# Token attention on one core: scores from stacked parts replaced by three passes over 32 partitions, two row tiles and two column tiles at a time

## The chip, the cores and the metric

One core of a Trainium2 chip runs the whole program. The metric is the device time in microseconds, as the median of several runs. The engines are TensorE (PE; its weight loads are listed apart as PEld), VectorE (DVE), ScalarE (ACT), GpSimd (POOL) and SyncE (SP), which issues the DMA transfers.

## What is computed

The input x has 64 batches of 96 channels by 512 tokens. The first part, which the change touches, is attention over tokens:

```python
q, k, v = jnp.split(qkv, 3, axis=1)                # 32 channels each
weight = jnp.einsum('bct,bcs->bts', q * scale, k * scale)
weight = jax.nn.softmax(weight, axis=-1)
h = jnp.einsum('bts,bcs->bct', weight, v)
```

Then follow a layer norm, a grouped-query attention with rotary embedding over the 32 channels as a sequence, and a feed-forward block with ternary weights, each added to h. These two blocks take about two thirds of the time and are the same in both kernels.

## The kernel before, in words

Token attention works on 16 groups (NG) of 4 batches (GB). Each batch has a 512 x 512 matrix of scores, cut into 4 tiles of 128 x 512, so a group has 16 tiles (STEPS). Every tile is computed twice. A **row tile** (rows, L622 to L628) has queries as rows; DVE takes the maximum of each row (maximum, L472 to L475) into one column of row_max. A **column tile** (cols, L635 to L643) is the transposed tile, keys as rows; ACT takes exp of it (exps, L421 to L435) into the ring E. Its matmul also subtracts the maximum of each query, so the exponentials need nothing but a scale.

Scores must be nearly fp32-exact while TensorE multiplies fp32r. So q and k are split into a high part (ACT, raise_, L413) and a low part (POOL, lower, L368). For each batch, three parts of 32 channels are stacked on 96 partitions, (high, high), (high, low), (low, high), in QP for queries and KP for keys. One matmul over 96 partitions then gives the whole sum. The stacking is done by DMA: stack(g), L270 to L282, copies the parts into every third partition of QP and KP, six transfers of 256 KB a group. Two more partitions of QP, 96 and 97, get the negative maxima, again as high and low part (store_max, L289 to L296); the same two partitions of KP hold ones (L565). So a column tile is one matmul over 98 partitions.

The maxima of a group travel so: when all 16 row tiles are reduced, TensorE transposes row_max (transpose_maxima, L630), DVE splits the result in max_hi and max_lo (take_transposed, L477), and SP stores both into QP. cols(g, 0) waits for that.

TensorE follows an order written out by hand (step, L686): in each of 16 steps of group g one row tile of group g+1 or g+2 and one column tile of group g or g+1. LOOK = 7 row tiles of a group are made ahead. At four steps (OUT_AT) comes weigh(g, i), L645: the exponentials of four batches times v, as matmuls with 32 output columns for each batch. Once a group comes total(g), L656: the sums of the exponentials, four sums of pairs from POOL (sum_pair, L373) and eight tiles of E, again with 32 output columns each.

The row tiles, the transposed maxima and the totals share a ring of NS = 3 PSUM banks (S, score_ring): entry n may start when entry n - 3 has been read (enter_ring, L617). Column tiles use three banks of their own (ST): tile n waits for exponential n - 3. The two outputs use the other two banks.

DVE also turns the totals (turn_sums), inverts them (invert, L492) and multiplies the output (finish, L499), at three steps after a total, and from group 8 on makes the weights of the feed-forward block ternary (below, above, L93 to L102) behind tiles 3 and 5. ACT measures weights in the first half (L437, L442) and splits those of the second attention from group 9 on (attn_high, L79), with POOL for the low parts (attn_low, L87). SP's queue carries everything in its order: the stacking of group g+2, the load of v, the loads of weights, the load of q and k of group g+3, the store of h and the store of the maxima.

Of the kernel before, what the change touches and what calls it, by code (L numbers as in the profile page):

```python
# [121 lines left out]
LOOK, TAKE = 7, 1  # L122
MAX_AT = 2 + STEPS - LOOK
DEN_AT = STEPS + 3
MEASURES_AT = {"fold": (8, 5), "spread": (8, 9), "last_sum": (13, 5)}


def score_ring():

    entries = [("row", 0, k) for k in range(STEPS)]  # L130
    for k in range(LOOK):
        entries += [("row", 1, k)] + ([("max", 0)] if k == TAKE else [])
    for g in range(NG):
        for u in range(2, STEPS + 2):
            if u < MAX_AT and g + 1 < NG:
                entries.append(("row", g + 1, u - 2 + LOOK))
            if u >= MAX_AT and g + 2 < NG:
                entries.append(("row", g + 2, u - MAX_AT))
            if u == MAX_AT + TAKE and g + 1 < NG:
                entries.append(("max", g + 1))  # L140
            if u + STEPS == DEN_AT and g > 0:
                entries.append(("den", g - 1))
            entries += [(what, 0) for what, at in MEASURES_AT.items() if at == (g, u)]
    entries.append(("den", NG - 1))
    return {entry: n for n, entry in enumerate(entries)}
# [8 lines left out]
NB, NV, NE, NS, NO = 3, 2, 3 * GB, 3, 2  # L154


class TokenTiles:

    def __init__(self, sb):
        parts = {}  # L160
        for n in (1, 2):
            parts["q", n] = sb(f"q_parts{n}", [P, GB, T], F32R)
            parts["k", n] = sb(f"k_parts{n}", [P, GB, T], F32R)
        self.qk = sb("qk_split", [P, 4, T])
        VT = {0: sb("v_t0", [P, NT, P])}
        for of in ("q", "k"):
            parts[of, 0] = sb(f"{of}_parts0", [P, GB, T], F32R)
# [3 lines left out]
        self.QP, self.KP = [parts["q", n] for n in range(NB)], [parts["k", n] for n in range(NB)]  # L171
# [13 lines left out]
def token_attention(nc, block, sem, tiles, W, rows1, qk_raw, vt, h1, tables_in, norm_in, mask_in, ident_in, w_attn,  # L185
                    w_ffn):

    with ExitStack() as ctx:
# [3 lines left out]
        QP, KP, VT, qk, E, SUM = tiles.QP, tiles.KP, tiles.VT, tiles.qk, tiles.E, tiles.SUM  # L192
# [15 lines left out]
        stacked = [sem(f"t_stacked{n}") for n in range(2)]  # L208
# [14 lines left out]
        COPIES = 6 * DMA  # L223
        SPLIT_AT = 13
# [8 lines left out]
        OUT_AT = {8: 0, 10: 1, 13: 2, 17: 3}  # L233
        def staged(g):

            return E[:, NE - 4:NE, :] if g == 1 else qk[:, :, :]

        def split_raw(g):
            return staged(g)[:, 0:2, :]

        def split_high(g):
            return staged(g)[:, 2:4, :].bitcast(F32R)

        def split_low(g):
            return staged(g)[:, 0:2, :].bitcast(F32R)

        def copies(g):
            return COPIES * (g // 2 + 1)

# [12 lines left out]
        def _(sp):  # L262
            def load_qk(g):
                if g == 2:
                    sp.wait_ge(stacked[0], copies(0))
                elif g > 2:
                    sp.wait_ge(stacked[(g - 1) % 2], copies(g - 1))
                sp.dma_start(split_raw(g), qk_raw[g, :, :, :]).then_inc(qk_in[g % 2], DMA)

            def stack(g):  # L270
                p, done = g % NB, stacked[g % 2]
                if g >= NB:
                    sp.wait_ge(st_done, STEPS * (g - NB + 1))
                sp.wait_ge(hi_done, g + 1)
                high, low = split_high(g).bitcast(FP32), split_low(g).bitcast(FP32)
                sp.dma_start(QP[p][0:3 * CH:3, :, :].bitcast(FP32), high[:, 0, :]).then_inc(done, DMA)
                sp.dma_start(KP[p][0:3 * CH:3, :, :].bitcast(FP32), high[:, 1, :]).then_inc(done, DMA)
                sp.dma_start(QP[p][1:3 * CH:3, :, :].bitcast(FP32), high[:, 0, :]).then_inc(done, DMA)
                sp.dma_start(KP[p][2:3 * CH:3, :, :].bitcast(FP32), high[:, 1, :]).then_inc(done, DMA)
                sp.wait_ge(lo_done, g + 1)  # L280
                sp.dma_start(QP[p][2:3 * CH:3, :, :].bitcast(FP32), low[:, 0, :]).then_inc(done, DMA)
                sp.dma_start(KP[p][1:3 * CH:3, :, :].bitcast(FP32), low[:, 1, :]).then_inc(done, DMA)  # L282
# [6 lines left out]
            def store_max(g):  # L289
                for part, of in enumerate((max_hi, max_lo)):  # L290
# [4 lines left out]
                    row = QP[g % NB][3 * CH + part:3 * CH + part + 1, :, :].bitcast(FP32)  # L295
                    sp.dma_start(row, of[:, :].bitcast(FP32)).then_inc(max_in, DMA)  # L296
# [11 lines left out]
            def convert_ffn(c):  # L308
                if c == 6:
                    sp.wait_ge(stacked[(NG - 1) % 2], copies(NG - 1))  # L310
# [15 lines left out]
            stack(0)  # L326
            load_qk(2)
            stack(1)
            load_v(0)
# [6 lines left out]
            for g in range(NG):  # L336
                if g + 2 < NG:
                    stack(g + 2)
# [28 lines left out]
        def _(pool):  # L367
            def lower(g):  # L368
                pool.wait_ge(hi_done, g + 1)
                nc.gpsimd.tensor_tensor(split_low(g), split_raw(g), split_high(g).bitcast(FP32), ALU.subtract  # L370
# [16 lines left out]
            for g in range(3):  # L387
                lower(g)
            for g in range(NG):
# [11 lines left out]
                if g + 3 < NG:  # L401
                    lower(g + 3)
# [1130 lines left out]
```

## Time and profile before

| | |
|---|---|
| Median of 3 runs | 1083.79 us (1079.22 to 1084.54) |
| The profiled execution: its own time | 1077.4 us |
| Its span, first to last instruction | 1075.6 us |
| PE busy in the span | 972.6 us (90%) |
| DVE / ACT / POOL busy | 736.6 / 446.2 / 497.7 us |
| Mean granted clock of TensorE | 0.976 |
| DMA moved | 113.07 MB |
| Token attention | from the start to about 332 us |

Times are in microseconds from the start of the span unless marked ns. In a timeline each line has the start, the busy time, engine, line of the kernel, operation, what is written from what, and the number of instructions merged into it; in brackets the idle time of the engine before it and who ended it. Successive matmuls overlap, so the distance between two starts is the cost of one in a stream, and its duration is how long it takes to end.

### The profile page before, as it was taken

How to read it: one execution, taken by the hardware profiler on the slowest of the kernel's cores; microseconds unless marked ns; L12 is line 12 of the kernel's file. 1: busy time of each engine (PE TensorE's matmuls, PEld its weight loads, DVE VectorE, ACT ScalarE, POOL GpSimd, SP SyncE). 2: the span in 40 equal slices, each digit the busy share in tenths (PEclk: the TensorE clock that was granted, in tenths of full speed). 3: DMA queues.
4: the chain of work that ended last, by engine and by line, in shares of the span. 5: the costliest groups of instructions: out<-in, count | busy, mean ns of one | idle time of the engine just before them, and what ended most of it. 6: DMA issues, size and time to landing. Idle time of an engine off the chain costs nothing. (4 is left out here: it accounts for less than half of the span.)

```text
span 1075.6 us, 20479 instructions
## 1 busy us (share of the span) xinstructions
PE 972.6 (90%) x7799; PEld 525.5 (49%) x7799; DVE 736.6 (68%) x1262; ACT 446.2 (41%) x761; POOL 497.7 (46%) x376
## 2 busy tenths in 40 slices
PE   4998999888887598999999999999999999999976
PEld 2433333333322245556566465564655656646545
DVE  5676758888797756567676685676856766668542
ACT  1677866677674522323333233232332333323311
POOL 2243434476677743634554355344553455435500
PEclk9999999999989699999999999999999999999998
DMA  8988886675524222322223123222232222322300
GB/s 220 268 289 229 284 248 186 192 212 180 171 94 112 51 59 44 80 49 54 69 49 78 49 49 80 48 67 59 54 78 51 51 68 49 78 52 46 73 16 21
DMA packets 157478, 113.07 MB, mean 105 GB/s; under 512 B 126336, under 2 KB 126976, under 8 KB 157440
## 3 DMA queue, kind: packets, MB, share of 16 engines
q1 hardware_dynamic: 157440, 112.59, 38.8%
q8 instruction: 21, 0.34, 0.1%
q14 instruction: 17, 0.14, 0.0%
HBM read 49.36 MB, written 8.39 MB: 54 GB/s over the span
## 5 line engine op out<-in xcount | busy, mean ns | idle before, releaser
L1007 POOL TENSOR_TENSOR roped<-rope_cos,rope_sin 128x512 f32<-128x512 f32 x80 | 100.8, 1268 | 222.1 <-DVE rope_sin L1173 222.1
L475 DVE TENSOR_REDUCE row_max<-score_rows 128x1 f32<-128x512 f32 x256 | 162.7, 677 | 46.8 <-PE score_rows L627 46.6
L435 ACT ACTIVATE exps<-score_cols 128x512 f32<-128x512 f32 x256 | 139.7, 600 | 82.8 <-PE score_cols L642 81.0
L1360 PE MATMUL ffn_sum<-x_hi,ffn_w 128*128 128x128 f16 x1408 | 165.0, 222 | 7.9 <-DMA x_lo<-x_lo_rows 7.9
L1361 PE MATMUL ffn_sum<-x_lo,ffn_w 128*128 128x128 f16 x1408 | 164.8, 222 | 0.0
L627 PE MATMUL score_rows<-k_parts,q_parts 96*128 96x512 f32 x256 | 120.1, 484 | 28.1 <-DMA k_parts<-qk_split 14.3
L1360 PEld LDWEIGHTS ffn_sum<-x_hi,ffn_w 128*128 128x128 f16 x1408 | 139.6, 99 | 11.7 <-DMA x_lo<-x_lo_rows 8.3
L1361 PEld LDWEIGHTS ffn_sum<-x_lo,ffn_w 128*128 128x128 f16 x1408 | 140.1, 99 | 1.8
L642 PE MATMUL score_cols<-q_parts,k_parts 98*128 98x512 f32 x256 | 107.3, 427 | 13.2 <-DMA q_parts<-max_lo 8.8
L379 POOL TENSOR_TENSOR exp_sums<-exps 128x512 f32<-128x512 f32 x64 | 83.3, 1330 | 57.7 <-PE score_rows L627 38.0
L627 PEld LDWEIGHTS score_rows<-k_parts,q_parts 96*128 96x128 f32 x256 | 51.4, 202 | 116.4 <-DVE row_max L475 65.4
L1019 POOL TENSOR_TENSOR roped_lo_rows<-roped,roped_hi_rows 128x512 f16<-128x512 f32 x80 | 94.5, 1197 | 15.7 <-ACT roped_hi_rows L1093 15.7
L1418 PE MATMUL proj<-attn_slots,ctx_hi 128*128 128x512 f16 x256 | 97.1, 379 | 3.5 <-POOL attn_slots L90 2.7
L1419 PE MATMUL proj<-attn_slots,ctx_hi 128*128 128x512 f16 x256 | 97.3, 380 | 0.0
L1295 DVE SCALAR_TENSOR_TENSOR h<-proj,o_unscale,h_res 128x512 f32<-128x512 f32 x16 | 12.0, 751 | 120.2 <-PE proj L1423 120.2
L852 POOL TENSOR_TENSOR rstd<-var,minus_half 128x1 f32<-128x1 f32 x32 | 23.7, 739 | 133.2 <-DVE var L847 133.2
L1073 ACT ACTIVATE squares<-ffn_sum 128x512 f32<-128x512 f32 x32 | 19.1, 597 | 149.2 <-PE ffn_sum L1309 149.2
L1307 PE MATMUL proj<-attn_slots,x_hi 128*128 128x512 f16 x192 | 73.5, 383 | 3.6 <-DMA x_lo<-x_lo_rows 3.6
L652 PE MATMUL tok_out<-exps,v_t 128*32 128x512 f32 x512 | 70.5, 624 | 3.5 <-ACT exps L435 3.4
L1308 PE MATMUL proj<-attn_slots,x_hi 128*128 128x512 f16 x192 | 73.5, 383 | 0.0
L1309 PE MATMUL proj<-attn_slots,x_lo 128*128 128x512 f16 x192 | 73.4, 382 | 0.0
L90 POOL TENSOR_TENSOR attn_slots<-attn_slots 128x1024 f16<-128x1024 f32 x20 | 47.3, 2364 | 52.5 <-ACT attn_slots L85 52.5
(153 smaller groups left out, 1931.1 us busy)
## 6 DMA issues: line engine op xcount, KB each, us to landing
q_parts<-qk_split SPq DMA_DIRECT2D x45, 256.0 KB, 4.2
k_parts<-qk_split SPq DMA_DIRECT2D x45, 256.0 KB, 4.7
attn_slots<-in_w_attn SPq DMA_DIRECT2D x20, 512.0 KB, 7.1
ffn_w<-in_w_ffn SPq DMA_DIRECT2D x13, 704.0 KB, 8.4
qk_split<-in_qk SPq DMA_DIRECT2D x15, 512.0 KB, 5.9
raw_ffn<-in_w_ffn SPq DMA_DIRECT2D x8, 704.0 KB, 5.3
v_t<-in_v_t SPq DMA_DIRECT2D x16, 256.0 KB, 5.7
h_rows<-tok_out_sum SPq DMA_DIRECT2D x16, 256.0 KB, 4.9
```

The source lines that it names most:

```text
L379: nc.gpsimd.tensor_tensor(SUM[:, b, :], E[:, first, :], E[:, second, :], ALU.add).then_inc(summed, 1)
L435: nc.scalar.activation(E[:, n % NE, :], ST[n % 3][:, :], ACT.Exp, scale=TOK_SCALE).then_inc(exp_done, 1)
L475: nc.vector.reduce_max(row_max[:, g % 2, k:k + 1], S[n % NS][:, :], AX.X).then_inc(s_free, 1)
L627: nc.tensor.matmul(bank[:, :], QP[g % NB][0:3 * CH, b, t * P:(t + 1) * P], KP[g % NB][0:3 * CH, b, :], start=True, stop=True).then_inc(s_f ...
L642: nc.tensor.matmul(ST[n % 3][:, :], KP[g % NB][0:3 * CH + 2, b, i * P:(i + 1) * P], QP[g % NB][0:3 * CH + 2, b, :], start=True, stop=True) ...
L1007: nc.gpsimd.tensor_tensor(rope[:, c, :], ra[c % 2][:, :], rb[c % 2][:, :], ALU.add).then_inc(added, 1)
L1019: nc.gpsimd.tensor_tensor(rope_lr[:, c, :], rope[:, c, :], rope_hr[:, c, :], ALU.subtract).then_inc(r_lo, 1)
L1307: nc.tensor.matmul(dst, ah, bh, start=(i == 0), stop=False)
L1360: nc.tensor.matmul(dst, w, x2h[:, k, :], start=(k == 0), stop=False)
L1361: ins = nc.tensor.matmul(dst, w, x2l[:, k, :], start=False, stop=(k == KD - 1))
L1418: nc.tensor.matmul(PROJ[1][:, :], ch[:, k, :], W.hi(at, D), start=(k == 0), stop=False)
L1419: nc.tensor.matmul(PROJ[1][:, :], ch[:, k, :], W.lo(at, D), start=False, stop=False)
```

## The change

- q and k are loaded with the 4 batches of a group on 32 partitions each (partition 32 b + channel), where before a partition held one channel of one batch in another order. The stacking, its tiles and its semaphore go. High and low parts stay in their own tiles, `high` and `low`, three of each in turn.
- A score tile is three accumulating matmuls over the 32 partitions of its batch: high x high, high x low, low x high. A column tile gets a fourth matmul over two partitions that adds the negative maxima: ones_r as weights, neg_max as the moving operand. The maxima are stored by DMA into partitions 0 and 1 of each batch's 32 in neg_max, which has two buffers.
- TensorE works in 8 windows a group instead of 16 steps. A window takes two row tiles of two neighbouring batches and two column tiles of the other two batches, and issues pass by pass over the four tiles. The waits for all four come ahead of the first matmul. The rings keep their three banks.
- Ahead of the column tiles are 8 row tiles (AHEAD = 4 pairs) instead of 7. The maxima of a group are transposed in window 5, the column tiles of the next group begin in window 8; weighings stand in windows 4, 5, 6 and, for the group before, 1; the total of the group before in window 2. The row tiles' order over batches changes with row_tile.
- ACT's raise and POOL's lower of a group come one group later than before (g+2 instead of g+3), behind exponential 3 and ahead of the sums. E has 16 tiles instead of 12. The raw q and k have two buffers.

```diff
+PAIRS = STEPS // 2
+AHEAD = PAIRS // 2
+MAX_AT, OUT_AT, DEN_AT = AHEAD + 1, {4: (0, 0), 5: (0, 1), 6: (0, 2), 1: (1, 3)}, 2
+def row_tile(j):
+    pair, second = divmod(j, 2)
+    i, half = divmod(pair, 2)
+    return 2 * half + second, i
+def rows_beside(g, w):
+    g, pair = (g + 1, w - 1 + AHEAD) if w < MAX_AT else (g + 2, w - MAX_AT)
+    return (g, pair) if g < NG else None
+def cols_at(g, w):
+    g, pair = (g, w) if w < PAIRS else (g + 1, 0)
+    return (g, pair) if g < NG else None
...
             def load_qk(g):
-                if g == 2:
-                    sp.wait_ge(stacked[0], copies(0))
-                elif g > 2:
-                    sp.wait_ge(stacked[(g - 1) % 2], copies(g - 1))
-                sp.dma_start(split_raw(g), qk_raw[g, :, :, :]).then_inc(qk_in[g % 2], DMA)
-            def stack(g):
...
+                if g >= 2:
+                    sp.wait_ge(lo_done, g - 1)
+                sp.dma_start(raw(g), qk_raw[g, :, :, :]).then_inc(qk_in[g % 2], DMA)
...
             def store_max(g):
+                if g >= 2:
+                    sp.wait_ge(st_done, STEPS * (g - 1))
...
-                    row = QP[g % NB][3 * CH + part:3 * CH + part + 1, :, :].bitcast(FP32)
-                    sp.dma_start(row, of[:, :].bitcast(FP32)).then_inc(max_in, DMA)
+                    sp.dma_start(neg_max[g % 2][part::CH, :].bitcast(FP32), of[:, :].bitcast(FP32)).then_inc(max_in, DMA)
...
             def raise_(g):
                 act.wait_ge(qk_in[g % 2], DMA * (g // 2 + 1))
...
+                if g >= NB:
+                    act.wait_ge(st_done, STEPS * (g - NB + 1))
+                nc.scalar.copy(high[g % NB][:, :, :], raw(g)).then_inc(hi_done, 1)
...
-            def rows(g, k):
...
-                nc.tensor.matmul(bank[:, :], QP[g % NB][0:3 * CH, b, t * P:(t + 1) * P], KP[g % NB][0:3 * CH, b, :],
-                                 start=True, stop=True).then_inc(s_full, 1)
+            def split_score(bank, g, b, i, of, n):
+                q, k = (0, 1) if of == "rows" else (1, 0)
+                p, at = g % NB, of_batch(b)
+                part, other = ((high, high), (high, low), (low, high))[n]
+                return nc.tensor.matmul(bank, part[p][at, q, i * P:(i + 1) * P], other[p][at, k, :], start=(n == 0),
+                                        stop=(of == "rows" and n == 2))
+            def scores(row_pair, col_pair):
+                rows, cols = [], []
+                if row_pair is not None:
+                    g, pair = row_pair
+                    if pair == 0:
+                        pe.wait_ge(lo_done, g + 1)
+                    for j in (2 * pair, 2 * pair + 1):
+                        rows.append((enter_ring(ring["row", g, j])[:, :], g, *row_tile(j)))
+                if col_pair is not None:
+                    g, pair = col_pair
+                    if pair == 0:
+                        pe.wait_ge(max_in, 2 * DMA * (g + 1))
+                    for u in (2 * pair, 2 * pair + 1):
+                        n = STEPS * g + u
+                        if n >= 3:
+                            pe.wait_ge(exp_done, n - 2)
+                        cols.append((ST[n % 3][:, :], g, u % GB, u // GB))
+                for n in range(3):
+                    for bank, g, b, i in rows:
+                        ins = split_score(bank, g, b, i, "rows", n)
+                        if n == 2:
+                            ins.then_inc(s_full, 1)
+                    for bank, g, b, i in cols:
+                        split_score(bank, g, b, i, "cols", n)
+                for bank, g, b, i in cols:
+                    of = slice(b * CH, b * CH + 2)
+                    nc.tensor.matmul(bank, ones_r[of, :], neg_max[g % 2][of, :], start=False, stop=True
+                                     ).then_inc(st_done, 1)
...
+            def step(g, w):
+                scores(rows_beside(g, w), cols_at(g, w))
+                if w == MAX_AT and g + 1 < NG:
                     transpose_maxima(g + 1)
+                if w in OUT_AT:
+                    back, i = OUT_AT[w]
+                    if g - back >= 0:
+                        weigh(g - back, i)
+                if w == DEN_AT and g > 0:
                     total(g - 1)
```

## Rows read from the trace of the kernel before

**Rows 1.** Waits of the whole span: engine, line, waited for; total, times, longest.
```profile
ACT exps L435 <- PE score_cols L642: 81.0, 64, 12.9
...
PEld score_rows L627 <- DVE row_max L475: 65.4, 100, 1.8
...
PEld score_cols L642 <- DMA q_parts<-max_lo: 17.4, 16, 2.5
```

**Rows 2.** Two windows: length, busy by engine, granted clock, DMA share, GB/s.
```profile
103.00:121.00 18.00, 17.07 (x102) 7.03 (x105) 13.15 (x24) 13.85 (x26) 7.37 (x5) 1.00 0.90 278
...
139.00:158.00 19.00, 16.41 (x81) 6.68 (x77) 12.53 (x22) 11.83 (x22) 7.37 (x5) 0.91 0.84 262
```

**Rows 3.** Timeline, TensorE: first column tiles of groups 0, 7, 15; one later matmul.
```profile
31.73 1.22 PE L642 MATMUL score_cols<-q_parts,k_parts 98*128 98x512 f32 x2 [1.95 <-DMA q_parts<-max_lo]
...
152.78 0.80 PE L642 MATMUL score_cols<-q_parts,k_parts 98*128 98x512 f32 x1 [1.85 <-DMA q_parts<-max_lo]
...
156.19 0.50 PE L627 MATMUL score_rows<-k_parts,q_parts 96*128 96x512 f32 x1
...
306.28 1.19 PE L642 MATMUL score_cols<-q_parts,k_parts 98*128 98x512 f32 x2 [1.41 <-ACT exps L435]
```

**Rows 4.** Timeline of group 4, TensorE and its weight loads.
```profile
102.15 0.19 PEld L627 LDWEIGHTS score_rows<-k_parts,q_parts 96*128 96x128 f32 x1
...
102.39 0.40 PE L627 MATMUL score_rows<-k_parts,q_parts 96*128 96x512 f32 x1
...
102.62 0.40 PE L642 MATMUL score_cols<-q_parts,k_parts 98*128 98x512 f32 x1
...
103.84 1.90 PE L664 MATMUL score_rows<-exps,tok_ones 128*32 128x512 f32 x16
...
105.67 0.50 PE L627 MATMUL score_rows<-k_parts,q_parts 96*128 96x512 f32 x1
...
111.10 0.39 PE L642 MATMUL score_cols<-q_parts,k_parts 98*128 98x512 f32 x1
...
112.42 0.50 PE L627 MATMUL score_rows<-k_parts,q_parts 96*128 96x512 f32 x1
...
117.00 0.50 PE L642 MATMUL score_cols<-q_parts,k_parts 98*128 98x512 f32 x1 [0.18 <-DMA q_parts<-max_lo]
```

**Rows 5.** DMA issues: count, KB each, median time to landing.
```profile
q_parts<-qk_split SPq DMA_DIRECT2D x45, 256.0 KB, 4.2
```

**Rows 6.** Lines of token attention, 0 to 340: count, busy us, mean ns, idle before.
```profile
L475 DVE TENSOR_REDUCE row_max<-score_rows 128x1 f32<-128x512 f32 x256 | 162.7, 677 | 46.8 <-PE score_rows L627 46.6
...
L435 ACT ACTIVATE exps<-score_cols 128x512 f32<-128x512 f32 x256 | 139.7, 600 | 82.8 <-PE score_cols L642 81.0 <-POOL exp_sums L379 0.6
...
L379 POOL TENSOR_TENSOR exp_sums<-exps 128x512 f32<-128x512 f32 x64 | 83.3, 1330 | 57.7 <-PE score_rows L627 38.0 <-ACT exps L435 14.8 <-PE score_rows L673 4.9
...
L84 ACT ACTIVATE attn_slots<-attn_slots,w_scale 128x1024 f16<-128x1024 f32 x16 | 18.3, 1146 | 7.7 <-POOL attn_slots L90 7.7
...
L101 DVE SCALAR_TENSOR_TENSOR ffn_w<-raw_ffn,w_thr,ffn_w 128x1408 f16<-128x1408 f32 x7 | 16.3, 2322 | 0.0
...
L96 DVE TENSOR_SCALAR ffn_w<-raw_ffn,w_nthr 128x1408 f16<-128x1408 f32 x7 | 10.1, 1448 | 0.0
```

**Rows 7.** Timeline of group 4, DVE.
```profile
107.02 0.23 DVE L494 RECIPROCAL tok_rden<-tok_den_t 128x16 f32<-128x16 f32 x1
...
107.92 0.65 DVE L475 TENSOR_REDUCE row_max<-score_rows 128x1 f32<-128x512 f32 x1
...
108.50 0.67 DVE L504 TENSOR_TENSOR tok_out_sum<-tok_out,tok_den_t 128x512 f32<-128x512 f32 x1
...
114.16 0.27 DVE L482 TENSOR_SCALAR max_hi<-score_rows 16x128 fp32r<-16x128 f32 x1
```

**Rows 8.** Timeline of the start, POOL and TensorE.
```profile
5.32 2.35 POOL L370 TENSOR_TENSOR qk_split<-qk_split 128x1024 fp32r<-128x1024 f32 x1 [4.88 <-ACT qk_split L419]
...
14.34 9.52 PE L627 MATMUL score_rows<-k_parts,q_parts 96*128 96x512 f32 x16 [14.34 <-DMA k_parts<-qk_split]
```

More of the change, by code:

```diff
@@ L151, in shares @@
     return [range(end - count, end) for count, end in zip(counts, ends)]
-NB, NV, NE, NS, NO = 3, 2, 3 * GB, 3, 2
+NB, NV, NE, NS, NO = 3, 2, STEPS, 3, 2
 class TokenTiles:
     def __init__(self, sb):
-        parts = {}
+        high, low, VT = {}, {}, {}
         for n in (1, 2):
[L162 to L167, printed above, removed]
+            high[n], low[n] = sb(f"qk_high{n}", [P, 2, T], F32R), sb(f"qk_low{n}", [P, 2, T], F32R)
+            if n == 1:
+                sb("tok_spare", [P, 4, T])
+        self.neg_max = [sb(f"neg_max{n}", [P, T], F32R) for n in range(2)]
+        self.ones_r = sb("tok_ones_r", [P, P], F32R)
+        sb("tok_spare2", [P, 2 * T - P])
+        self.qk = sb("qk_raw", [P, 4, T])
+        VT[0] = sb("v_t0", [P, NT, P])
+        high[0], low[0] = sb("qk_high0", [P, 2, T], F32R), sb("qk_low0", [P, 2, T], F32R)
         self.E = sb("exps", [P, NE, T])
@@ L170, in __init__ @@
         VT[1] = sb("v_t1", [P, NT, P])
-        self.QP, self.KP = [parts["q", n] for n in range(NB)], [parts["k", n] for n in range(NB)]
+        self.high, self.low = [high[n] for n in range(NB)], [low[n] for n in range(NB)]
         self.VT = [VT[n] for n in range(NV)]
@@ L232, in token_attention, with raw, of_batch @@
         SUMS_BEFORE = [sum(GB * d for d in DEPTH[:g]) for g in range(NG + 1)]
[L233 to L248, printed above, removed]
+        def raw(g):
+            return qk[:, 2 * (g % 2):2 * (g % 2) + 2, :]
+        def of_batch(b):
+            return slice(b * CH, (b + 1) * CH)
         def ffn_stage(c):
@@ L385, in sum_third @@
                 nc.gpsimd.tensor_tensor(SUM[:, b, :], SUM[:, b, :], E[:, third, :], ALU.add).then_inc(summed, 1)
-            for g in range(3):
-                lower(g)
+            lower(0)
+            lower(1)
             for g in range(NG):
+                if g + 2 < NG:
+                    lower(g + 2)
                 for c in A_CONVERTED[g][:1]:
@@ L445, in sum_ffn @@
                                      ).then_inc(f_stat, 1)
-            for g in range(3):
-                raise_(g)
+            raise_(0)
+            raise_(1)
             exps(0, 0)
@@ L471, in _, with maximum @@
         def _(dve):
-            def maximum(g, k):
-                n = ring["row", g, k]
+            def maximum(g, j):
+                n = ring["row", g, j]
+                b, i = row_tile(j)
+                k = b * NT + i
                 dve.wait_ge(s_full, n + 1)
```

152 lines of the change are left out of this document (49 added, 103 removed).

## The prediction

> **What bounds it now.** I read first the waits, then the windows, then the costs of one instruction, and last the timeline of one group. The waits show no single master: the loads of row tiles wait 65.4 us for DVE's maxima, the exponentials wait 81.0 us for TensorE's column tiles, and TensorE waits on the row of maxima that a DMA brings (17.4 us on the weight load) [rows 1]. The windows show a full machine: in 18 us of one group TensorE has records for 17.07 us, ACT for 13.85, DVE for 13.15, and the DMA engines are busy 0.90 [rows 2]. The stage is thus a loop of three engines with TensorE a little ahead. Its pace: the first column tile of group 0 starts at 31.73, that of group 7 at 152.78, that of group 15 at 306.28 [rows 3]: 17.3 us a group over seven groups, then 19.2 over eight.
>
> In the timeline, scores follow each other every 0.235 us at full clock (102.39 to 102.62), and the next weights are loaded meanwhile. One lasts 0.40, or 0.50 after an idle moment, so 0.10 of its load is then exposed. A weighing (eight records) adds 112.42 - 111.10 - 0.235 = 1.08, a total adds 105.67 - 102.62 - 0.235 = 2.82 [rows 4]. TensorE's own work per group is so 32 x 0.235 + 4 x 1.08 + 2.82 + 0.24 (the transposition, one pitch, an estimate) = 14.9 of 17.3 us. The tiles of 32 output columns share TensorE: 16 records in 1.90 us [rows 4]; rows of 32 partitions side by side are not in this trace.
>
> **The change, part by part.**
>
> 1. Copies. 96 transfers of 256 KB leave SP's queue, 25 MB in all [rows 5]. TensorE's waits on DMA inside the stage are mostly for the maxima, which stay. ACT's raise and POOL's lower keep their size. Lower now stands before the sums, which cost 4 x 1330 ns [rows 6]; they have until step 2 of the next group, four windows or over 8 us, so I cost that at nothing. Without that cover it is 2.4 us a group. SP's new wait for the column tiles of a group that is long finished, before the store of the maxima, costs nothing; so does ACT's before the raise.
>
> 2. Passes. Four tiles need 3 rounds of four matmuls plus one round of two that adds the maxima, where there were 4 matmuls of 0.235. If the four row groups run side by side, a window (two row tiles, two column tiles) is 0.10 + 4 x 0.235 = 1.04 us, against 0.94. That is no saving, and per group 0.8 us more. Lower bound for a round: 0.235; upper: four or two matmuls one after another, 14 x 0.235 = 3.29 a window. I take the lower, since the nearest row, with column tiles, shows four at once.
> The Trainium skill (TensorE: Matmul & The Clock Gate, Part 3) gives 3.07 times for four row tiles of 512 columns instead of 4; by that a round would be an estimated 0.31 and the sum some 37 us longer. It also says that weight loads overlap running matmuls only in other row groups; the load at 102.15 inside a matmul over the same rows disagrees.
>
> 3. Coupling, the term that decides. The rings stay at three banks, but a window takes two of each. Its second tile may start only when the first tile of the window before has been reduced, and the same holds for the exponentials. Before, a ring of three let TensorE run ahead by a tile at a time. In a window begun at 0: row tiles are full at 0.50 + 2 x 0.235 = 0.97, column tiles, one round later, at 1.21. With handovers of 0.04 to 0.05 (107.02 + 0.23 to the next, an estimate for all [rows 7]) the first maximum (677 ns [rows 6]) frees TensorE at 1.74 and the first exponential (600 ns) at 1.90. A plain window takes 1.90, not the 0.94 that TensorE used before. With a weighing TensorE is the limit: 2.12. With a total: 3.86.
>
> 4. DVE in windows 3 and 4. The inversion takes 0.90 of DVE (107.02 to 107.92) and the finish 0.60, the pitch of the maximum before it (107.92 to 108.50) [rows 7]; they now stand between tiles 12 and 13 and behind 13. From window 3's start: tile 12 at 1.01, inversion, tile 13 at 2.53, finish, tile 14 at 3.75, done 4.42. Window 5 starts at 4.5 rather than 4.02.
> A group: 2.12 + 3.86 + 4.5 + (2.12 + 0.23) + 2.12 + 1.90 + 1.90 = 18.75.
> The maxima: taken about 2.5 us into window 5; store and landing took 117.00 - 114.43 = 2.6 [rows 4, 7]; window 8 begins 6.4 after window 5, so that wait (17.4 us on the weight loads [rows 1]) should vanish. The sum has it already, since 18.75 holds no such wait.
>
> 5. Late groups 8 to 13. DVE's two conversions (1448 and 2322 ns [rows 6]) follow tiles 3 and 5, each the last of a pair. TensorE has only one window in hand, so they hold windows 8 and 1: by the same steps 1.95 us. ACT's two conversions (two operations of 1146 ns each [rows 6]) behind tiles 3 and 12 add about 0.4: 21.1 a group.
>
> 6. Start. The lowering of group 0 ends at 5.32 + 2.35 = 7.7 and rows start there rather than at 14.34. But TensorE is at half clock then (16 tiles in 9.52 us, DVE-paced, 0.60 apart [rows 8]). A pair at that clock: 0.79 + 2 x 0.43 = 1.65 to full, 0.7 for the maximum and its handovers: 2.4. Twelve pairs: 28.8, so first columns at 36.5 instead of 31.73, +5.
>
> Sum: +5; groups 0 to 6: 7 x 18.75 - 121.05 = +10; one more for the first group at half clock; groups 7 to 14: 2 x 18.75 + 6 x 21.1 - 153.5 = +11; the last group is bounded by ACT and DVE in both, 0. That is +27 us at full clock.
>
> 7. Clock. At 152.78, after 1.85 us without work, a matmul takes 0.80; at 156.19 one takes 0.50 again [rows 3], and that stretch has a granted clock of 0.91 (the other shown 1.00) [rows 2]: 3.4 us at the lower of the two levels, 1.2 and 2.4 GHz. In plain windows TensorE now streams 0.94 of 1.90 us, two or three in a row. I take one such fall a group, at 1.2 us on the path: +18. Ends: 0, or two falls wholly on the path, +50.
>
> Total +45: 1077.4 + 45 = 1122. The profiled run is 6.4 below the median 1083.79, so 1129 beside the median; I say 1128. The bounds of steps 3 and 7 reach from +15 to +90.
>
> **Rivals.**
>
> A. Forecast, slower by 2 to 7%: 0.60.
>
> B. The row groups don't run fully side by side: loads of the same array rows, or outputs into four banks, serialize. With rounds of 0.43 (each load of 0.19 exposed [rows 4]) a window grows by some 0.65, 5 us a group, 1128 + 80 = 1208; wholly serial, 2.35 a window less the idle 0.9 where there is some, 16 a group: 1128 + 250 = 1380. By the skill's 3.07, 1165. For: no row shows four row groups. Against: the column tiles. Chance 0.18 (0.08 up to 1195, 0.10 above). In this rival the change doesn't do what "side by side" says.
>
> C. Faster. The copies are what holds the stage (DMA 0.90 busy), so that with them gone no engine waits and TensorE's own work decides. Its price per group is then 8 x 1.04 + 4 x 1.08 + 2.82 + 0.24 = 15.7; against 17.3 and 19.2 (there DVE keeps it near 17.5), and a start some 6 us earlier: -11 - 14 - 6 = -31, about 1053. It decides if plain windows take under 1.5 us. For: the DMA share, the waits on maxima. Against: in the timeline the engines wait for each other, not for a copy, and the ring needs the first maximum. Chance 0.13.
>
> D. No change: DVE and ACT are a tenth quicker with less traffic and the clock holds: a plain window of 1.7, 17.6 a group, the start's loss made good: 1084. Chance 0.09.
>
> **Numbers.** A measurement of this kernel can tell about 0.5% from no change (1078.4 to 1089.2). Faster 0.13, same 0.09, slower 0.78. The range 1080 to 1195 leaves out C (0.13) and the upper part of B (0.10), a little over 2 in 10; A's own range is 1098 to 1165.
>
> **What would show it.** Step 1: the q_parts and k_parts issues gone, DMA share near 0.6. Step 2: matmuls of 32 rows starting some 10 ns apart in fours, rounds 0.235 apart. Step 3: starts of plain windows 1.9 apart, idle of TensorE put down to exponentials rather than maxima, and column tiles of neighbouring groups 18 to 19 us apart early, 21 late. Step 4: tile 14 of a group waits behind the finish. Step 6: first columns near 36.5. Step 7: PEclk under 0.95 in slices 2 to 12. The forecast is wrong if rounds are over 0.3 apart (B) or if the stage's column tiles end before 320 (C).

## The result, and the profile after

The changed kernel takes 1142.12 us (median of 4 runs, 1139.12 to 1145.1) beside 1082.01 for the kernel before on the same chip: a ratio of 1.0556, 95% interval 1.0514 to 1.0598. It is slower by 60 us, where 45 were forecast, within the range. The profiled execution has a span of 1140.5 us against 1075.6.

The page of the changed kernel: span, busy tenths of TensorE, its granted clock and the DMA share in 40 slices.

```profile
span 1140.5 us, 23159 instructions
...
PE   4788888887778967999999999999999999999986
...
PEclk9999899788887587999999999999999999999998
DMA  3235351233114231322322312322322322222210
```

The granted clock is below 9 tenths in ten of the first sixteen slices (mean of the span 0.943, before 0.976), and 88 MB are moved instead of 113. The first slices need care: the granted clock of the start reads 1.00,

```profile
0.00:36.09 36.09, 18.42 (x69) 9.81 (x69) 14.51 (x26) 3.37 (x3) 4.86 (x6) 1.00 0.37 130
```

but the durations of its matmuls (0.79, and rounds 0.43 apart) are those of the lower level until 53.5. In the start the level is therefore read from durations. The waits, answering to [rows 1]:

```profile
ACT exps L423 <- PE score_cols L651: 169.6, 108, 31.3
...
PEld score_rows L621 <- DVE row_max L465: 125.3, 96, 2.5
...
PE score_rows L621 <- ACT exps L423: 31.6, 36, 1.7
```

ACT now waits 169.6 us for column tiles instead of 81.0, the row tiles' weight loads wait 125.3 us for maxima instead of 65.4, and a wait is there that had no such row: row tiles that wait 31.6 us for exponentials. A window needs both rings. The pace, against [rows 3], by the first column tiles of groups 0, 7 and 15:

```profile
36.09 0.79 PE L621 MATMUL score_cols<-qk_high 32*128 32x512 f32 x2
...
177.45 0.50 PE L621 MATMUL score_cols<-qk_high 32*128 32x512 f32 x2
...
364.29 0.79 PE L621 MATMUL score_cols<-qk_high 32*128 32x512 f32 x2 [1.70 <-ACT exps L423]
```

| | before | after | difference |
|---|---|---|---|
| first column tile, group 0 | 31.73 | 36.09 | +4.4 |
| groups 0 to 6 | 121.05 (17.3 each) | 141.36 (20.2 each) | +20.3 |
| groups 7 to 14 | 153.50 (19.2 each) | 186.84 (23.4 each) | +33.3 |
| group 15 and all that follows | 769.3 | 776.2 | +6.9 |

The last line is the rest of each span. Its 6.9 are +11.4 in group 15, whose last pair of column tiles starts at 390.74, 26.5 us after its first (before 321.38, 15.1 us after), and -4.5 behind it.

One group in the timeline of TensorE, windows 3 and 4 of a group, and its last windows and the next window 1:

```profile
125.31 0.50 PE L621 MATMUL score_rows<-qk_high 32*128 32x512 f32 x2
125.32 0.50 PE L621 MATMUL score_cols<-qk_high 32*128 32x512 f32 x2
125.65 0.39 PE L621 MATMUL score_rows<-qk_low,qk_high 32*128 32x512 f32 x1
...
126.12 0.40 PE L651 MATMUL score_cols<-neg_max,tok_ones_r 2*128 2x512 f32 x2
127.30 0.49 PE L621 MATMUL score_rows<-qk_high 32*128 32x512 f32 x2 [0.78 <-ACT exps L423]
...
128.43 1.07 PE L666 MATMUL tok_out<-exps,v_t 128*32 128x512 f32 x8
129.89 0.49 PE L621 MATMUL score_rows<-qk_high 32*128 32x512 f32 x2 [0.39 <-DVE row_max L465]
...
136.35 0.50 PE L621 MATMUL score_rows<-qk_high 32*128 32x512 f32 x2 [0.78 <-ACT exps L423]
...
138.33 0.51 PE L621 MATMUL score_rows<-qk_high 32*128 32x512 f32 x2 [0.76 <-ACT exps L423]
...
138.92 0.63 PE L621 MATMUL score_cols<-qk_high,qk_low 32*128 32x512 f32 x2
...
139.90 1.94 PE L666 MATMUL tok_out<-exps,v_t 128*32 128x512 f32 x8
141.77 0.73 PE L621 MATMUL score_rows<-qk_high 32*128 32x512 f32 x2
```

Row and column tiles start within 0.01 us, the next round 0.34 later and the one for the maxima 0.81 later, as three rounds of 0.235 and the 0.10 that the first load adds. The window from 125.31 to 127.30 is a plain one: 1.99. Two more stand at 136.35 and 138.33, 1.98 apart. In the second the clock falls, after two idle stretches of TensorE of 0.78 and 0.76: a matmul lasts 0.63 and rounds are 0.43 apart, the weighing takes 1.94 instead of 1.07, until 0.73 at 141.77 is the last long one. DVE in the same group, against [rows 7]:

```profile
126.31 0.69 DVE L465 TENSOR_REDUCE row_max<-score_rows 128x1 f32<-128x512 f32 x1
126.92 0.24 DVE L484 RECIPROCAL tok_rden<-tok_den_t 128x16 f32<-128x16 f32 x1
...
127.83 0.65 DVE L465 TENSOR_REDUCE row_max<-score_rows 128x1 f32<-128x512 f32 x1
128.41 0.67 DVE L494 TENSOR_TENSOR tok_out_sum<-tok_out,tok_den_t 128x512 f32<-128x512 f32 x1
129.00 1.27 DVE L465 TENSOR_REDUCE row_max<-score_rows 128x1 f32<-128x512 f32 x2
```

The inversion (126.92) stands between the maxima of tiles 12 and 13 and the finish (128.41) behind 13; tile 14 comes at 129.00, and window 5 starts at 129.89, 4.58 after window 3, not when the weighing of window 4 is over (128.43 + 1.0). The windows of groups without and with a fall, and of the last group:

```profile
97.60:116.60 19.00, 16.30 (x173) 7.13 (x169) 12.85 (x22) 13.99 (x25) 7.38 (x5) 1.00 0.42 151
116.60:137.20 20.60, 17.88 (x175) 7.52 (x169) 12.85 (x22) 13.06 (x23) 7.38 (x5) 0.92 0.44 164
364.20:392.80 28.60, 27.00 (x120) 10.30 (x120) 14.67 (x22) 12.68 (x20) 14.11 (x9) 0.56 0.28 70
```

19.0 us at full clock, 20.6 with a fall (0.92), and in the last group a granted clock of 0.56 with TensorE 94% busy. By the distance of first column tiles, group 0 took 22.7 us (at the lower level until 53.5), groups 1 to 3 took 19.0, groups 4 to 7 20.5, and groups 8 to 14 between 21.4 and 26.1.

### The profile page after: what moved, and what is told of

It reads as the page before. It is cut to its first block and busy times, and to the rows that moved or that the text cites. A ratio compares the mean times of both kernels' runs of the same rounds, so it can differ in the third digit from the quotient of the medians.

```text
span 1140.5 us, 23159 instructions
## 1 busy us (share of the span) xinstructions
PE 1017.8 (89%) x9079; PEld 549.2 (48%) x9079; DVE 730.8 (64%) x1260; ACT 448.5 (39%) x761; POOL 487.7 (43%) x376
## 3 DMA queue, kind: packets, MB, share of 16 engines
HBM read 49.36 MB, written 8.39 MB: 51 GB/s over the span
## 5 line engine op out<-in xcount | busy, mean ns | idle before, releaser
L465 DVE TENSOR_REDUCE row_max<-score_rows 128x1 f32<-128x512 f32 x256 | 165.5, 683 | 106.6 <-PE score_rows L621 104.9
L423 ACT ACTIVATE exps<-score_cols 128x512 f32<-128x512 f32 x256 | 140.3, 595 | 169.8 <-PE score_cols L651 169.6
L621 PE MATMUL score_rows<-qk_high 32*128 32x512 f32 x256 | 73.7, 563 | 70.4 <-ACT exps L423 31.6
L362 POOL TENSOR_TENSOR qk_low<-qk_raw,qk_high 128x1024 fp32r<-128x1024 f32 x16 | 38.0, 2379 | 181.4 <-ACT qk_high L409 181.4
L621 PEld LDWEIGHTS score_rows<-qk_high 32*128 32x128 f32 x256 | 29.5, 209 | 167.4 <-DVE row_max L465 125.3
L666 PE MATMUL tok_out<-exps,v_t 128*32 128x512 f32 x512 | 85.4, 746 | 1.2 <-ACT exps L423 1.2
L861 POOL TENSOR_TENSOR rstd<-var,minus_half 128x1 f32<-128x1 f32 x32 | 22.7, 710 | 133.4 <-DVE var L856 133.4
L1082 ACT ACTIVATE squares<-ffn_sum 128x512 f32<-128x512 f32 x32 | 19.1, 597 | 151.8 <-PE ffn_sum L1318 151.8
L621 PE MATMUL score_cols<-qk_high 32*128 32x512 f32 x256 | 72.2, 560 | 3.2 <-ACT exps L423 3.2
```

The lines of the kernel that those rows point to most:

```text
L423: nc.scalar.activation(E[:, n % NE, :], ST[n % 3][:, :], ACT.Exp, scale=TOK_SCALE).then_inc(exp_done, 1)
L465: nc.vector.reduce_max(row_max[:, g % 2, k:k + 1], S[n % NS][:, :], AX.X).then_inc(s_free, 1)
L621: return nc.tensor.matmul(bank, part[p][at, q, i * P:(i + 1) * P], other[p][at, k, :], start=(n == 0), stop=(of == "rows" and n == 2))
L666: last = nc.tensor.matmul(OUT[g % NO][b * CH:(b + 1) * CH, :], VT[g % NV][:, i, b * CH:(b + 1) * CH], E[:, (STEPS * g + GB * i + b) % NE, ...
```

## The experiments

Every run stands beside runs of the kernel before on the same chip (medians 1076.6 to 1080.7), so runs from different chips are compared by ratio; the changed kernel has 1.0556. What is said of single groups rests on one trace of each kernel.

### The clock

Extra matmuls, which change nothing in the output, into the output bank that is free until the next weighing:

```diff
+            def fill(g, count):
...
+                if g >= NO:
+                    pe.wait_ge(h_done, g - NO + 1)
+                for _ in range(count):
+                    nc.tensor.matmul(OUT[g % NO][:, :], ones_r[:, 0:P], ones_r[:, :], start=True, stop=True)
...
                 scores(rows_beside(g, w), cols_at(g, w))
+                if w in (7, 8):
+                    fill(g + 1, 3)
+                if w == 3 or g == 0 and w < 3:
+                    fill(g, 3)
...
                 scores((0, pair), None)
+                fill(0, 3)
```

> The changed kernel with extra matmuls into an output bank that is free at that time (three of 512 columns, weights and operand all ones, behind the windows of the start, behind windows 7, 8 and 3, and 1 and 2 of the first group); what is computed stays the same. Theory: the clock fell once a group because TensorE idles 0.9 of 1.98 us in plain windows, and it was low through the start for the same reason. Then the granted clock of token attention is near 1.0, early groups take 19.0 instead of 20.5 us, a pair of the start 1.8 instead of 2.5, the first column tiles start near 29 instead of 36; in all 1110 (1100 to 1122) against 1142. Rival: the low stretches are hidden behind DVE and ACT, or the extra matmuls cost what they give: only the start gains, 1133 or more.

Measured: 1117.55, ratio 1.0362 (1.0314 to 1.0411). Every group from 1 to 7 took 19.1 us, without a fall. But the start got longer. Its timeline, and for comparison that of the changed kernel:

```profile
7.73 0.79 PE L621 MATMUL score_rows<-qk_high 32*128 32x512 f32 x2 [7.73 <-POOL qk_low L362]
...
9.30 1.65 PE L660 MATMUL tok_out<-tok_ones_r 128*128 128x512 f32 x3
10.88 0.79 PE L621 MATMUL score_rows<-qk_high 32*128 32x512 f32 x2
...
14.03 0.79 PE L621 MATMUL score_rows<-qk_high 32*128 32x512 f32 x2
```

```profile
8.18 0.79 PE L621 MATMUL score_rows<-qk_high 32*128 32x512 f32 x2 [8.18 <-POOL qk_low L362]
...
10.57 0.79 PE L621 MATMUL score_rows<-qk_high 32*128 32x512 f32 x2 [0.75 <-DVE row_max L465]
...
13.09 0.79 PE L621 MATMUL score_rows<-qk_high 32*128 32x512 f32 x2 [0.87 <-DVE row_max L465]
```

A pair takes 3.15 us with the extra matmuls and 2.49 without. TensorE had no pause between 7.73 and 14.03, and yet every duration is that of the lower level, and stays so until past 62 us (53.5 in the changed kernel). So "it idles, hence the low clock", as the expectation had it for the start, is refuted there: the first column tiles came at 45.78, where 29 was expected. The same without them in the start:

> As the kernel with extra matmuls, but none in the start (there the clock stayed low in spite of them, and a pair took 3.15 instead of 2.49 us): only behind windows 7, 8 and 3, and 1 and 2 of the first group. Theory (one fall of the clock a group in the plain windows, another stretch in the last group): 10 less than with them in the start, 1107 (1103 to 1112). Rival (what that kernel gained came from the clock having been raised in the start): the falls come back, 1125 or more.

Measured: 1112.03, ratio 1.0322 (1.0283 to 1.0361). Two windows of it, an early and a late group:

```profile
99.00:118.10 19.10, 18.77 (x184) 8.43 (x178) 12.84 (x22) 13.99 (x25) 7.40 (x5) 1.00 0.44 149
255.90:277.20 21.30, 18.98 (x184) 8.64 (x178) 16.87 (x25) 14.81 (x23) 11.60 (x8) 1.00 0.33 119
```

No fall in either, nor in any other group. Against 1.0556 the falls are worth some 25 us, and rather more, since the extra matmuls have a cost of their own (19.1 against 19.0 in a group without a fall). The first group stays long, 24.1 us. In the two traces the falls are worth 1.4 to 1.5 in each of groups 4 to 7, 19 in groups 8 to 14 together, and 10 in the last one alone, which shrank from 26.5 to 16.4 us.

### The pairs and the rings

One output bank (control), the bank that is freed so given to the row ring, and the same bank given to the column tiles. The control has NO = 1. The second run has NS = 4 besides, the third NST = 4, the number of banks for column tiles. The edit of the third run:

```diff
-NB, NV, NE, NS, NO = 3, 2, STEPS, 3, 2
+NB, NV, NE, NS, NO = 3, 2, STEPS, 3, 1
+NST = 4
...
-        ST = [pb(f"score_cols{n}") for n in range(3)]
+        ST = [pb(f"score_cols{n}") for n in range(NST)]
...
-                nc.scalar.activation(E[:, n % NE, :], ST[n % 3][:, :], ACT.Exp, scale=TOK_SCALE).then_inc(exp_done, 1)
+                nc.scalar.activation(E[:, n % NE, :], ST[n % NST][:, :], ACT.Exp, scale=TOK_SCALE).then_inc(exp_done, 1)
...
-                        if n >= 3:
-                            pe.wait_ge(exp_done, n - 2)
-                        cols.append((ST[n % 3][:, :], g, u % GB, u // GB))
+                        if n >= NST:
+                            pe.wait_ge(exp_done, n - NST + 1)
+                        cols.append((ST[n % NST][:, :], g, u % GB, u // GB))
```

> The changed kernel with one output bank instead of two, a control for the next two. The weighing of window 4 now waits until DVE has finished the group before, about 1 us after it would start. Both theories: 0.5 to 1.5 us a group and something at the end, 1155 (1145 to 1170).

> One output bank, and the freed bank goes to the ring of row tiles: four instead of three, so a window of row tiles needs only that the window before the last has been reduced. Theory (coupling of pairs to the ring): plain windows stay at 1.98 since the exponentials free them, but window 4 no longer waits for the finish and the late groups no longer wait for the two conversions: 10 to 25 us less than with one output bank alone. Rival (TensorE's own rounds or the clock set the pace): within 4 us of it.

> One output bank, and the freed bank goes to the column tiles: four instead of three. Theory: plain windows are freed by the first maximum then, 1.78 instead of 1.98, four or so a group: 8 to 14 us less than with one output bank alone; in the last group, which has column tiles only, TensorE alone sets the pace. Rival (TensorE's own rounds or the clock set the pace): within 4 us of it.

Measured: the control 1149.12, with four row banks 1124.77, with four column banks 1138.92, all on one chip and beside 1079.09. The row bank gives 24 us, the column bank 10. Of the 24, about 10 are the start: the first round for the maxima of column tiles comes at 27.3 us instead of 37.2. The column bank does what was expected in plain windows, and loses in late groups. Two window starts of the kernel with four column banks in the timeline of TensorE, and one late group in the windows:

```profile
63.56 0.50 PE L622 MATMUL score_rows<-qk_high 32*128 32x512 f32 x2
...
65.37 0.51 PE L622 MATMUL score_rows<-qk_high 32*128 32x512 f32 x2 [0.60 <-DVE row_max L466]
```

```profile
242.80:269.00 26.20, 22.03 (x173) 9.13 (x169) 15.81 (x25) 14.89 (x23) 10.75 (x7) 0.74 0.26 97
```

The window is 1.81 instead of 1.98, the first maximum now being what frees it. A late group takes 26.2 us with a clock of 0.74. Both banks moved the time by as much as the coupling theory said, and neither could have if TensorE's rounds were the bound.

The reverse: the kernel before, with nothing but waits added.

```diff
+            def ahead(g, u):
+                at = (g + 1, u - 2 + LOOK) if u < MAX_AT else (g + 2, u - MAX_AT)
+                if at[0] < NG:
+                    pe.wait_ge(s_free, ring[("row",) + at] - NS + 1)
+                n = STEPS * g + u
+                if n < STEPS * NG and n >= 3:
+                    pe.wait_ge(exp_done, n - 2)
             def step(g, u):
+                if u % 2 == 0:
+                    ahead(g, u + 1)
```

> The kernel before with waits added alone: ahead of every second step TensorE also waits for what the next step needs, so that it moves by two row and two column tiles as the changed one does; matmuls, copies and rings as before. Theory (moving by pairs in rings of three banks costs time by itself): a plain pair takes 1.43 instead of 0.94 us, less than the 1.98 of the changed kernel since its tiles end one after another; a group grows by 0.5 to 1.5 us, 1079 to 1095 (1087 to 1103). Rival (the coupling costs nothing; the fourth round and the clock are the whole loss): within 4 of 1079.

Measured: 1131.56, ratio 1.0552 (1.0471 to 1.0633): as slow as the change, with the old matmuls, the old copies and stacks. The expectation, 1095 and at most 1103, was 37 us short.

A pair of row tiles and the next in the timeline of TensorE, and the window of an early group:

```profile
111.65 0.50 PE L627 MATMUL score_rows<-k_parts,q_parts 96*128 96x512 f32 x1
...
113.93 0.47 PE L627 MATMUL score_rows<-k_parts,q_parts 96*128 96x512 f32 x1 [1.07 <-DVE row_max L475]
```

```profile
157.50:177.90 20.40, 17.85 (x91) 7.14 (x89) 12.91 (x22) 13.16 (x24) 7.58 (x6) 0.92 0.78 243
```

The pair begun at 111.65 holds until 113.93, 2.28 us, where 1.43 were expected. The profile names a maximum that had long been done; what ended last is an exponential, since ACT had a bound and its raise (110.78 to 113.23 in its timeline) around the exponential before. In a ring that TensorE fills tile by tile such a piece of work is absorbed; waiting for two at once it is not. And this kernel too has a fall of the clock in every group from 1 to 13, as in the window above (0.92), where the kernel before has three in the whole stage. Its granted clock is 0.955; how much of its 55 us is clock was not tried. All of them are lost in groups 0 to 14: the first column tile starts at 31.5, and the last group takes 14.9, both as before.

### The rounds

One pass instead of three, so that the low parts of the scores are left out:

```diff
-                part, other = ((high, high), (high, low), (low, high))[n]
-                return nc.tensor.matmul(bank, part[p][at, q, i * P:(i + 1) * P], other[p][at, k, :], start=(n == 0),
+                return nc.tensor.matmul(bank, high[p][at, q, i * P:(i + 1) * P], high[p][at, k, :], start=True,
...
-                for n in range(3):
+                for n in (2,):
```

> The changed kernel with one of the three passes (high times high) and the round for the maxima: two rounds a window instead of four; the scores leave out the low parts. Theory (the window is a chain: rounds, then the first maximum or exponential, then the next window): every round taken away shortens plain windows by its 0.235, 1.98 to 1.5, a pair of the start from 2.49 to 1.65, a group from 20.5 to 16 or so; in all 1077 (1065 to 1100). Rival (DVE and ACT set the pace and the rounds hide behind them): 1120 or more.

Measured: 1110.77, ratio 1.0331 (1.0283 to 1.0378): 24 us by ratio, not 65. Two window starts, and a late group:

```profile
123.43 0.50 PE L620 MATMUL score_rows<-qk_high 32*128 32x512 f32 x2 [0.76 <-ACT exps L423]
...
124.95 0.49 PE L620 MATMUL score_rows<-qk_high 32*128 32x512 f32 x2 [0.78 <-ACT exps L423]
```

```profile
247.70:271.10 23.40, 18.17 (x109) 5.24 (x105) 16.32 (x25) 14.94 (x24) 11.80 (x8) 0.67 0.28 108
```

The plain window did shrink to 1.52, and the start by 10 us. But TensorE, with less to do, was at the lower level for longer: granted clock 0.911 over the span, 0.67 in a late group of 23.4 us, and 0.76 from the first to the last column tile, where the changed kernel has 0.88. That the clock took what the missing rounds gave fits these rows, but it is argued and not shown, since this kernel was not tried with the extra matmuls.

The same matmuls with the three passes of a tile one behind the other in the queue:

```diff
-                for n in range(3):
-                    for bank, g, b, i in rows:
+                for bank, g, b, i in rows:
+                    for n in range(3):
...
-                    for bank, g, b, i in cols:
+                for bank, g, b, i in cols:
+                    for n in range(3):
```

> The changed kernel with the same matmuls in another order: the three passes of one tile, then those of the next, so that neighbours in the queue use the same 32 rows. Theory (four row groups really work at once, and the queue is served in order): ten rounds instead of four, a window of 2.45 instead of 1.04 us of TensorE, some 6 us more a group, 1240 (1215 to 1265). Rival (the records only start together and the work is the same): within 10 of 1142.

Measured: 1154.33, ratio 1.0738 (1.0698 to 1.0779). The theory's 100 us are not there, and the time is 12 us above 1142, just outside what the rival gave. The records show that the order in the queue was not the order of work:

```profile
153.54 0.51 PE L621 MATMUL score_rows<-qk_high 32*128 32x512 f32 x2
153.56 0.51 PE L621 MATMUL score_cols<-qk_high 32*128 32x512 f32 x2
153.88 0.39 PE L621 MATMUL score_rows<-qk_low,qk_high 32*128 32x512 f32 x2
...
154.12 0.40 PE L621 MATMUL score_rows<-qk_high,qk_low 32*128 32x512 f32 x2
```

In the queue the first tile's three passes stand ahead of all the others. On the engine the first passes of all four tiles start together, within 0.04 us from 153.54, then the second passes, then the third: the second tile's first matmul ran ahead of the first tile's second. Groups 1 to 3 take 19.1 us, about as before. By its trace the 12 to 20 us are lost in late groups above all (groups 7 to 14 took 198.6 us instead of 186.8), whose clock fell for longer; that cause is not settled.

This gives a remedy: if order in the queue doesn't matter, each tile's waits can stand ahead of its own matmuls.

```diff
                     for j in (2 * pair, 2 * pair + 1):
...
+                        bank = enter_ring(ring["row", g, j])[:, :]
+                        for n in range(3):
+                            ins = split_score(bank, g, *row_tile(j), "rows", n)
+                        ins.then_inc(s_full, 1)
...
                         if n >= 3:
                             pe.wait_ge(exp_done, n - 2)
...
+                        bank, b = ST[n % 3][:, :], u % GB
+                        for part in range(3):
+                            split_score(bank, g, b, u // GB, "cols", part)
...
```

> The changed kernel with the matmuls tile by tile, and each tile's waits ahead of its own matmuls instead of all waits ahead of the window (matmuls and rings as in the changed kernel; the run with the tiles one after another in the queue showed that TensorE still runs them side by side, if nothing waits between them). Theory (the loss is that a window waits for four banks at once): a tile starts when the tile three before it has been read, as in the kernel before; a pair of the start takes 1.6 instead of 2.5 us, a group 1.5 to 2.5 less; 1100 (1080 to 1118). Rival (the fourth round and the clock are the loss, or waits between tiles keep them from running side by side): 1145 or more.

> The same with the extra matmuls behind windows 7, 8 and 3 (and 1 and 2 of the first group). Theory: coupling and clock are separate losses, so that this takes off another 15 to 30: 1080 (1065 to 1098), near the kernel before. Rival (they are one loss: with the waits apart TensorE has no idle stretch that lowers the clock): within 6 of the run without them.

Measured: 1132.91, ratio 1.0496 (1.0454 to 1.0538), and with the extra matmuls 1106.54, ratio 1.0237 (1.0177 to 1.0298).

```profile
92.50:111.20 18.70, 18.70 (x174) 10.03 (x171) 12.84 (x23) 14.10 (x25) 7.39 (x5) 1.00 0.44 152
254.60:279.30 24.70, 22.93 (x172) 11.03 (x170) 16.80 (x25) 14.85 (x24) 11.55 (x8) 0.79 0.27 102
```

The first expectation, 1100, failed by 33 us. The start did what was expected: three row tiles every 2.43 us, 1.62 a pair, and the first maxima round at 28.0 instead of 37.5. But that is all that was gained. Groups 2 to 7 take 18.6 without a fall, 0.4 less than 19.0 where 1.5 to 2.5 were expected, and late ones take 24.7 at a clock of 0.79. The first two row tiles of a window 8 show why:

```profile
90.97 0.39 PE L621 MATMUL score_rows<-qk_high 32*128 32x512 f32 x1
91.20 0.40 PE L621 MATMUL score_rows<-qk_low,qk_high 32*128 32x512 f32 x1
91.44 0.39 PE L621 MATMUL score_rows<-qk_high,qk_low 32*128 32x512 f32 x1
91.65 0.50 PE L621 MATMUL score_rows<-qk_high 32*128 32x512 f32 x1
```

The tile starts at 90.97, 1.06 us after window 7 instead of 1.98, but the other three wait for their banks, and it has its three rounds to itself, as long as those of four tiles. The next starts at 91.65. By the start of window 2 little is left of the lead: window 1, again with a lone tile, takes 2.96 instead of 2.13, and windows 7, 8 and 1 together take 5.82 instead of 6.08. TensorE now has records for all of the 18.70 us and is by them the limit. Tiles that start one by one lose the side-by-side work that makes three passes as cheap as one.

The extra matmuls take off 26, within the 15 to 30 expected, so the two losses are separate; but the 1080 was missed by 27 as the run without them missed its 1100. With the extra matmuls the records fill all 19.1 us of an early group, so that less of them might do better. No kernel tried here beats the one before.

### Two smaller steps

The copies, put back for 12 groups into a tile that nobody reads:

> The changed kernel with the six copies a group put back for 12 of 16 groups (256 KB each, into a tile that nobody reads, from SP's queue at their old place). Theory (the copies were hidden): 1142 (1136 to 1149). Rival (the copies slowed the other engines or the loads, and the change gained something by leaving them out): 1155 or more.

Measured: 1138.47, ratio 1.0569 (1.0529 to 1.061), against 1.0556: 72 transfers, 19 MB, are worth nothing that can be measured in the changed kernel, where nothing on TensorE waits for them.

DVE's inversion and finish moved out of window 3's pair, in the kernel with extra matmuls:

```diff
-                    if j == row_before("den") + 1 and r >= 2:
+                    if j == row_before("den") + 2 and r >= 2:
                         invert(r - 2)
-                    if j == row_before("den") + 2 and r >= 2:
+                    if j == row_before("den") + 4 and r >= 2:
                         finish(r - 2)
```

> The changed kernel with extra matmuls behind windows 7, 8 and 3 (its early groups took 19.1 us each, with no fall of the clock), and on DVE the inversion moved from behind row tile 12 to behind 13 and the finish from behind 13 to behind 15: no work of DVE stands inside window 3's pair any more. Theory (the inversion and the finish hold window 5 by half a microsecond): early groups 18.6 to 18.7, in all 5 to 8 less than the 1112 without the move. Rival (window 5 is freed by the exponentials and TensorE's weighing anyway): groups stay at 19.1.

Measured: every group from 1 to 7 took 18.7 instead of 19.1 us, as expected. One of them:

```profile
96.70:115.40 18.70, 18.70 (x179) 8.43 (x178) 12.81 (x23) 13.97 (x26) 7.41 (x5) 1.00 0.43 153
```

In all it is 1111.42, ratio 1.0271 (1.0221 to 1.0322), and that interval reaches the 1.0322 of the kernel without the move, so the total doesn't show the gain. In the trace the last group took 21.2 instead of 16.4 us, with a fall of the clock that the other kernel has not; the extra matmuls do not keep the clock up there in every kernel.

## Why the prediction was right, by its steps

1. **Copies at nothing: right.** Their return cost nothing measurable, and the lowering ahead of the sums delayed nobody: window 2 with its total took 3.85 in an early group, the 3.86 of the sum. The DMA share fell further than the 0.6 that was named as a sign, to 0.42.
2. **Rounds: right.** Four row groups work side by side, 0.235 a round. The 3.07 times that the Trainium skill (TensorE: Matmul & The Clock Gate, Part 3) gives would have made rounds of an estimated 0.31; the trace has 0.23. The same part of the Trainium skill has the rule that weight loads overlap only with other row groups' matmuls, and it did not hold here either, as in the rows before: a round of 0.235 would have no room for a load of 0.19 in the same rows if the load had to wait. Rival B is out.
3. **Coupling: right in mechanism and size.** Plain windows 1.98 (forecast 1.90), early groups 19.0 at full clock (18.75), and window by window 2.13, 3.85, 1.98 + 2.59, 2.35, 2.13, 1.97, 1.98 against 2.12, 3.86, 4.5, 2.35, 2.12, 1.90, 1.90. One more row bank and one more column bank moved the time as this step says, and so did the waits added to the kernel before, which cost far more than worked out. Waits by tile did so in the start alone. Both sides of the coupling are thus needed for the account: four tiles must start together for the passes to be cheap, and rings of three banks do not let four start together without waiting.
4. **DVE in windows 3 and 4: right.** 0.4 us a group, by the run that moves it.
5. **Late groups: right at full clock.** In the kernel with extra matmuls behind the windows alone, without falls, groups 8 to 13 took 19.9 to 22.1 us, 21.0 on average; forecast 21.1. Group 14 took 20.9, where the forecast had 18.75, and no run takes the two conversions apart.
6. **Start: right, in part by luck.** 36.09 against 36.5; a pair 2.49 against 2.4. But rows start at 8.18 and not at 7.7, and the first column tiles start together with the twelfth pair, so eleven pairs lie ahead of them and not twelve; with eleven the forecast's own price gives 34.1. The transposition's 0.6, which it left out, and the dearer pairs made up for that. The "one more for the first group at half clock" was too small: group 0 took 22.7 us, 3.7 more than the next three, since the lower level lasted until 53.5.
7. **Clock: the term that was mis-sized.** "One such fall a group, at 1.2 us on the path: +18". Groups 1 to 3 had none (the first stands at 118 us, the forecast's sign had them from slice 2 on), groups 4 to 7 one each at 1.5 us. Late groups had more and longer low stretches, and the last group had a granted clock of 0.56. The run with extra matmuls behind the windows alone puts the falls at some 25 us or a little more, and the forecast's 0 for the last group was wrong by 11.4, of which those matmuls took away 10.

Groups 0 to 6 with the start were forecast at 5 + 10 + 1 and 8 for the clock, 24, and measured 24.7; there the long first group and the missing falls of groups 1 to 3 cancel. Groups 7 to 14 were forecast at 11 + 10 and measured 33.3: there lies the difference. The rival "faster" had the DMA share as its evidence; it fell from 0.9 to 0.4 and neither DVE nor ACT ran noticeably quicker (a maximum 683 ns, before 677; an exponential 595, before 600).

## What to carry to other kernels

If several tiles are issued as one unit, count the banks: a ring of n banks taken k at a time leaves n - k in hand, and short work of the readers between two tiles, which a ring taken one by one absorbs, then stops the producer. The waits alone cost the kernel before 55 us. Each tile's wait ahead of its own matmuls is no way out where the gain comes from tiles that start together: here it helped the start and nothing else. And a change that makes TensorE wait more often can cost more than the waits: look at the granted clock of the stretch, and at the durations of matmuls, before counting the gain.

## What was not expected of the hardware

TensorE did not keep to the order of its queue between 32-row groups: with three passes of one tile queued ahead of the next tile's, the four tiles' first passes still started within 0.04 us. In the start of the kernel with extra matmuls there, TensorE worked without a pause from 7.73 us on, on two row groups of four and on full-height matmuls with operands of ones, from 49.36 on with column tiles on all four, and its durations stayed those of the lower level past 62 us; in the kernel before, the matmuls of 96 rows from 31.73 on went from 0.63 at 35.74 to 0.40 at 36.85. And in the last group of the changed kernel, whose windows hold column tiles alone, the granted clock was 0.56 with TensorE 94% busy. Idle stretches are thus not all that goes with the lower level. What makes the difference was not tried.
